# A short add in place of a pow between the two row scatters of each expert tile on GpSimd

## What is computed

```python
logits = x2 @ router_w
probs = jax.nn.softmax(logits, axis=-1)
top_p, top_e = jax.lax.top_k(probs, K)             # K = 2 of 8 experts
...
h = h + jnp.where(m, jax.nn.gelu(xd @ w_in[e] + b_in[e]), 0.0)
...
y = y + jnp.where(m, h @ w_out[e] + b_out[e], 0.0)
...
y = y * sp[:, None]
out = jnp.zeros((T, Dm), x.dtype).at[st].add(y)
```

## Time and profile before

| | |
|---|---|
| median of 3 runs | 477.92 us (474.49 to 478.58) |
| the profiled execution | 474.49 us, of which the span of the trace is 472.6 us |
| PE busy | 394.9 us (84%) |
| DVE busy | 368.8 us (78%) |
| ACT busy | 331.4 us (70%) |
| POOL busy | 268.7 us (57%); of it pauses (L778) 54.7 us in 71, scatters of the expert stage (L771) 81.4 us in 78 |

### The profile page before, as it was taken

The page is one execution under the profiler, slowest core; times in us unless marked ns, Lnnn a source line. Parts: engine busy times, 40 slices in busy tenths (PEclk is TensorE's granted clock), DMA queues, the critical chain, the costliest instruction groups (busy, mean ns, idle before and its releaser), DMA issues.

```text
span 472.6 us, 13099 instructions
## 1 busy us (share of the span) xinstructions
PE 394.9 (84%) x4092; PEld 308.3 (65%) x4092; DVE 368.8 (78%) x1416; ACT 331.4 (70%) x671; POOL 268.7 (57%) x313
## 2 busy tenths in 40 slices
PE   2758899998999989999899987789559999979850
PEld 1536667776776777677686765568438897967740
DVE  2888888998988889899789786367655667779994
ACT  2855788898889889898879877566706666646640
POOL 2522112545454364626545565769988888888870
PEclk9998999999999999999999999899959999999996
DMA  7245576664565555875553774624335569396985
GB/s 242 83 139 163 180 214 179 196 181 141 177 213 170 166 171 167 221 204 184 180 174 111 223 220 121 198 68 130 101 126 143 170 175 332 116 341 251 323 275 204
DMA packets 69500, 87.10 MB, mean 184 GB/s; under 512 B 9485, under 2 KB 55290, under 8 KB 69306
## 3 DMA queue, kind: packets, MB, share of 16 engines
q1 hardware_dynamic: 60074, 65.81, 46.7%
q0 software_dynamic: 6816, 18.65, 10.8%
q10 hardware_dynamic: 2544, 1.81, 1.2%
HBM read 51.07 MB, written 35.18 MB: 182 GB/s over the span
## 4 chain that ended last, share of the span: by engine, by line
PE 42%; POOL 17%; issue 14%; DVE 10%; DMA 8%; ACT 6%; ACTq 0%; POOLq 0%; DVEq 0%; SPq 0%
PE ps_J L1650 12%; PE ps_F L1650 6%; POOL store_y L771 6%; DMA store_y<-y_out,y_row 6%; PE ps_O L1764 5%; PE ps_T L1659 5%; POOL store_x L765 5%; PE ps_S L1751 5%; POOL pause_t L778 5%; PE ps_R L1689 2%; PE ps_O L1775 2%; PE ps_G L1650 2%; DMA temp_t<-in_temp 1%; DVE y_out L2934 1%; DVE xb_lo L2903 1%
## 5 line engine op out<-in xcount | busy, mean ns | idle before, releaser
L771 POOL DMA_INDIRECT store_y<-y_out,y_row x78 | 81.4, 1044 | 21.8 <-issue 16.5
L765 POOL DMA_INDIRECT store_x<-xn_E,slot_u x64 | 68.0, 1063 | 26.5 <-DVE slot_u L2633 13.6
L1089 ACT ACTIVATE prob<-ps_S 128x512 f32<-128x512 f32 x128 | 72.4, 594 | 12.7 <-PE ps_S L1751 10.0
L778 POOL TENSOR_TENSOR pause_t<-half_ones,minus_half 128x2 f32<-128x2 f32 x71 | 54.7, 770 | 1.9
L1751 PE MATMUL ps_S<-q_stack,k_stack 128*128 128x256 f16 x256 | 44.5, 276 | 5.9 <-issue 3.8
L2922 DVE TENSOR_TENSOR h_lo<-h_f,h_hi 128x512 f16<-128x512 f32 x39 | 26.9, 689 | 21.0 <-ACT h_hi L1173 9.4
L1650 PE MATMUL ps_J<-wout_hi,h_hi 128*128 x112 | 31.2, 278 | 14.3 <-DVE y_out L2934 10.9
L1764 PE MATMUL ps_O<-prob,v_wide 128*32 128x128 f32 x1024 | 41.0, 279 | 1.1 <-ACT prob L1089 0.5
L1165 ACT ACTIVATE h_f<-ps_F,bin_t 128x256 f32<-128x256 f32 x56 | 23.4, 470 | 24.5 <-PE ps_F L1650 18.9
L751 POOL TENSOR_TENSOR rstd_C<-var_C,minus_half 128x2 f32<-128x2 f32 x16 | 12.1, 759 | 40.4 <-DVE var_C L2412 40.4
L1650 PE MATMUL ps_F<-xb_hi,win_hi 128*128 128x256 f16 x112 | 31.7, 283 | 3.9 <-DVE xb_lo L2903 3.3
(11 more groups left out here) (301 smaller groups left out, 1399.5 us busy)
## 6 DMA issues: line engine op xcount, KB each, us to landing
parts_scratch<-parts SPq DMA_DIRECT2D x32, 256.0 KB
k_stack<-parts_scratch SPq DMA_DIRECT2D x64, 128.0 KB
q_stack<-parts_scratch SPq DMA_DIRECT2D x128, 64.0 KB
xb<-store_x SPq DMA_DIRECT2D x30, 257.0 KB
y_got<-store_y SPq DMA_DIRECT2D x14, 512.0 KB
c_in<-in_ctx SPq DMA_DIRECT2D x16, 256.0 KB
x_in<-in_x SPq DMA_DIRECT2D x16, 256.0 KB
store_x<-zeros SPq DMA_DIRECT2D x15, 257.0 KB, 4.6
```

The costliest lines, as they stand in the source:

```text
L765: pool.indirect_dma_start(store_x, bass.IndirectOffsetOnAxis(slot_u[q][:, at:at + 1], 0), xn_e[q][:, at, :], None).then_inc(s_scat[q], 16)
L771: pool.indirect_dma_start(store_y, bass.IndirectOffsetOnAxis(y_row[n][:, b:b + 1], 0), y_out[n][:, b, :], None).then_inc(s_y_kept[n], 16)
L778: pool.tensor_tensor(pause_t[:, :], half_ones[:, :], minus_half[:, 0:2], ALU.pow).then_inc(s_set_p, 1)
L1089: act.activation(prob[m % PROBS][:, 2 * n:2 * n + 2, :, :], bank_s[n], ACT.Sigmoid, scale=float(HD) ** -0.5).then_inc(s_prob[n], 1)
```

## The change

In the loop over tiles 4 to 38, the pause between the two scatters of a tile (there is one for tiles 4 to 35, 32 in all) becomes another instruction of the same engine and size. Before, it is a `pow` of 128x2 elements with the inputs `half_ones` and `minus_half`; now it is an `add` of 128x2 elements whose two inputs are both `minus_half`. It still writes `pause_t`, still waits for the pause before it and still raises the same semaphore. The 39 pauses outside of the loop stay as they are, and so do the order of instructions and all waits of every engine. No pause stands between the second scatter of a tile and the first of the next, before or after.

```diff
+            def pause():
+                pool.wait_ge(s_set_p, next(paused))
+                pool.tensor_tensor(pause_t[:, :], minus_half[:, 0:2], minus_half[:, 0:2], ALU.add).then_inc(s_set_p, 1)
 
             def long_pause():
                 pool.wait_ge(s_set_p, next(paused))
...
             for i in range(4, TILES):
                 keep_block(i, 0)
                 if i < CLOSE:
-                    long_pause()
+                    pause()
                 keep_block(i, 1)
```

## The result

The kernel with the add takes 481.21 us in the median of 20 runs (476.05 to 488.40), that of before 477.06 us (473.29 to 481.57, 20 runs). The ratio is 1.0077, 95% interval 1.0051 to 1.0102: slower by 0.8%, where I forecast a gain of 0.7%.

The account below looks back on a forecast made before the run. PE was taken to bound 385 to 416 us and DVE 416 to 457 us, with GpSimd felt only through scatter landings. Gains of 2.5 + 0.8 = 3.3 us took the 477.92 us median to 474.6 us, range 470.5 to 481.5 us.

Parts of the forecast that it names:

- The pause: Tiles 4 to 35 on GpSimd: the add takes 0.25 us (0.10 to 0.45), each pause 0.48 us shorter than the pow.
- The backlog, the landing, the stretch that VectorE bounds: GpSimd's 1.4 us backlog goes, scatters land 1.9 us earlier, take_rows and add_pair waits vanish after 416 us: 2.5 us gained.
- the sum: Whole kernel: 2.5 us from VectorE's stretch plus 0.8 us from PE's, 3.3 us faster.
- Rival A: Landings don't follow the earlier issue of scatters, the 1.53 us take_rows wait stays: about 1 us gained, 476.9 us; chance 0.20.
- The stretch that PE bounds: 385 to 416 us: take_rows waits that delay h_lo and leave PE idle go, 0.8 us gained (0.5 to 1.1).
- tiles 8 to 16: Part of tiles 4 to 16: take_rows waits for no scatter after tile 8, GpSimd gains only idle time: nothing.
- rival B: GpSimd's earlier scatters or adds hold up DVE's two-input instructions, some 0.6 us a tile over twelve tiles: 482 us; chance 0.15.
- Rival C: GpSimd's add takes as long as the pow, 0.73 us, so nothing changes: 477.9 us; chance 0.05.
- D: More than the sum: PE's whole 1.1 us, uncounted gaps around waits, backlog elsewhere: 5 us or more, 472.5 us; chance 0.12.
- The other direction of that wait: DVE's h_lo holds up a GpSimd pause started behind it (1.24 us in one case); the sum took nothing for this.

Follow-up runs that it names:

- spare_pow: act_stores plus, in tiles 16 to 35, two unread GpSimd scatters of 8 bytes a row with the pow between: 480.26 us, 1.0055 to the kernel of before.
- spare_add: act_stores plus, in tiles 16 to 35, two unread GpSimd scatters of 8 bytes a row with one add between: 484.99 us, 1.0177 to the kernel of before.
- act_stores: No GpSimd scatters of the experts' output or pauses between; ScalarE's queue writes the same bytes to consecutive rows: 463.26 us, 0.9703 to the kernel of before.
- late_add: Kernel of before with the pow kept up to tile 26 and the add from tile 27 on: 476.84 us, 0.9976 to the kernel of before.
- early_add: Reverse order: the add up to tile 26, the pow from tile 27 on: 488.54 us, 1.0221 to the kernel of before.
- act_stores_pow: act_stores plus two GpSimd pows after each y_out from tile 4 on: 462.57 us, 0.9687 to the kernel of before.
- yb7_add: The changed kernel (add) with seven buffers for y_out and y_row instead of five: 481.73 us, 1.0069 to the kernel of before.
- yb7_pow: The kernel of before (pow) with seven buffers for y_out and y_row instead of five: 476.89 us, 0.9995 to the kernel of before.
- pow_then_add: Kernel of before with the pow kept up to tile 21 and the add from tile 22 on: 477.45 us, 1.0033 to the kernel of before.

## Why the prediction was wrong

**The pause.** I took 0.25 us, between 0.10 and 0.45. Measured 0.20 us where nothing meets it, 0.36 in the median, 0.34 in the mean (10.9 us for 32). Within my bounds; a pause is 0.38 us shorter on average and not 0.48.

**The backlog, the landing, the stretch that VectorE bounds.** Right in the main. The distance to y_out is 0.28 us (forecast 0.27), the loads of y_got come 2.0 us earlier against y_out of tile 24 (forecast about 2), the take_rows waits are gone after 385 us. Tiles 26 to 38 take 2.9 us less, where the sum had 2.5. VectorE's own share did not rise to the 95% that I named: it is busy 37.9 of 41 us as before. Rival A falls with the landings.

**The stretch that PE bounds.** This step failed, and with it the sign of the sum. It said that PE gains 0.8 us there, "between 0.5 and 1.1", since its only losses were those behind take_rows. For tiles 8 to 16 it said "What GpSimd gains is idle time: nothing". The profile after loses 2.0 us in tiles 8 to 16 and 2.9 us in 16 to 26. I had taken GpSimd's work as something that others feel only through the landing of its scatters ("whoever needs it does so through the landing"). They feel its issuing too: the pow was not idle filling but what kept the second scatter at a distance from the first. For the signals the runs show it by presence (lags appear with the first scatter in spare_pow and spare_add, and vanish without scatters in act_stores) and by dose (12 and 13 signals over 1.45 us late with no add and one, 6 and 1 with two and three). For the time they show it by place (late_add 0.9976, early_add 1.0221) and by the chains of waits; by dose only in part, since tiles 8 to 26 take 67.6, 63.3, 63.3 and 59.0 us. How much of the 4.9 us each late signal costs is not shown.

That 481.21 us lies within my range, which ended at 481.5, is luck: its upper end was drawn for rival B, by a mechanism that the runs don't have.

**The trace of before had it.** Of 42 signals matched there, 12 come over 0.5 us late, up to 1.36 us. One case: the transposes into ps_T are done at 388.19, counted as above, and ACT's xb_hi, which waits for them, starts at 389.57. The timeline puts this down to PE:

```profile
389.57 0.60 ACT L1152 ACTIVATE xb_hi<-ps_T 128x512 f16<-128x512 f32 x1 [1.28 <-PE ps_T L1826]
```

I read it as PE being late. All stay within what PE has in stock, it seems, and no name looked odd.

**Rival B** ended on the right side for a wrong reason. h_lo is 0.69 us long as before in the median, and pows on GpSimd without scatters cost VectorE nothing (act_stores_pow): GpSimd does not hold it up. Its 482 us is near the measured 481.21 by chance. **Rival C** is refuted (the add took 0.20 us where nothing met it), and so is **D** (5 us or more won).

**The other direction of that wait** does matter. An add that starts while an h_lo runs takes until its end. VectorE's and GpSimd's timelines:

```profile
369.40 0.69 DVE L2926 TENSOR_TENSOR h_lo<-h_f,h_hi 128x512 f16<-128x512 f32 x1 [0.58 <-ACT h_hi L1177]
```

```profile
369.42 0.72 POOL L778 TENSOR_TENSOR pause_t<-minus_half 128x2 f32<-128x2 f32 x1
372.58 0.20 POOL L778 TENSOR_TENSOR pause_t<-minus_half 128x2 f32<-128x2 f32 x1
```

The add ends at 370.14, 0.05 us behind h_lo. A held add acts like a pow: the pair starts 1.87 us apart (the add at 369.42), where that of the next tile (372.58) starts 1.35 us apart. From 350 to 424 us 7 of 21 adds were held to 0.38 us or more in the trace of after, 4 of 19 in that of early_add. That two kernels with the same program up to tile 26 lose 4.9 and 11.5 us in tiles 8 to 26 could come of such chances of phase. I didn't test it, and why early_add is so much slower is open. The Trainium skill, "SBUF — State Buffer", section "SBUF: two separate sides", calls the ports that the two share an exclusive lock for whoever starts first. The trace agrees for this order, with 0.72 us for the add instead of 0.20, as it did before for a pow.

**What stays open.** By which path a scatter that is being issued keeps TensorE's signals back, no run shows. The same section of the Trainium skill says that, among the engines, only that shared pair causes contention and that TensorE never waits on anyone. The traces don't contradict it: TensorE itself runs on, with matmuls up to 374.41 in the case above, while its signal of 372.77 is out until 374.54. What the hold costs alone, without any change in landings, no run shows cleanly; the nearest is the 4.9 us in tiles 8 to 26 of after.

## What to carry to other kernels

A cheap instruction between two DMAs that GpSimd issues may be there for the distance and not for its result: before shortening it, look up how long after their last matmul TensorE's consumers start, and whether they start late while such DMAs are issued. Give the scatters room (some 1.9 us from start to start here) where TensorE sets the pace, and pack them where VectorE does; here that was worth 0.24% (late_add), at the edge of what the runs can tell. A queue that runs behind is not mended by more buffers: they hide one wait and bring up the next one that stands on the same queue.

## What the runs showed of the hardware

- TensorE's end-of-group signals came 0.17 to 0.18 us after the last matmul without scatters (act_stores), up to 1.36 us with the pair 1.9 us apart (before), up to 2.94 us with the pair 1.35 us apart (after, early_add), and 6.96 us in one case of a queue that hardly rested (yb7_add). Rows of 8 bytes gave the same lateness as rows of 1 KB (1.33 and 2.83 us, spare_pow and spare_add).
- Behind a scatter that started over 1.6 us after the one before it, 1 signal of 34 was over 0.5 us late; behind one that followed closer, 38 of 65 (before, late_add, yb7_pow).
- GpSimd's add of 128x2 f32 took 0.20 us, its pow of the same shape 0.73 us; scatters without anything between them start 1.26 us apart.
- In pow_then_add an idle time of 2.63 us of PE inside a busy stretch was followed by about 4 us at a granted clock of 0.57, with matmuls of 0.42 us instead of 0.27: there the hold cost more than its length.
